# Edge features stored by the counting stage and loaded by the message stage of a graph network kernel

## The reference

```python
def _mlp(h, W, b, gamma, beta):
    h = jax.nn.relu(h @ W + b)
    mu = jnp.mean(h, axis=0)
    var = jnp.mean(jnp.square(h - mu), axis=0)
    return gamma * (h - mu) * jax.lax.rsqrt(var + EPS) + beta
node_feat = _mlp(x, W_node, b_node, g_node, beta_node)
edge_feat = _mlp(edge_attr, W_edge, b_edge, g_edge, beta_edge)
row, col = (edge_index[0], edge_index[1])
message = jnp.concatenate([x[row], x[col], edge_feat], axis=1)
message = _mlp(message, W_msg, b_msg, g_msg, beta_msg)
agg = jax.ops.segment_sum(message, col, num_segments=node_feat.shape[0])
return agg + node_feat
```

## Time and profile before

| | |
|---|---|
| median of 3 runs | 2815.78 us (2812.81 to 2824.91) |
| profiled execution | 2801.42 us, of which the span is 2799.7 |
| count_edges | about 57 to 600 us |
| pass_messages | about 1403 to 2621 us |
| busy share of the span | PE 66%, DVE 56%, POOL 33%, ACT 31% |
| mean granted clock of TensorE | 0.735 |

### The profile page before, as it was taken

The page is one execution under the profiler, slowest core; times in us unless marked ns, Lnnn a source line. Parts: engine busy times, 40 slices in busy tenths (PEclk is TensorE's granted clock), DMA queues, the critical chain, the costliest instruction groups (busy, mean ns, idle before and its releaser), DMA issues. The chain is left out here.

```text
span 2799.7 us, 50246 instructions
## 1 busy us (share of the span) xinstructions
PE 1853.1 (66%) x14611; PEld 1446.8 (52%) x14611; DVE 1564.5 (56%) x4031; ACT 861.7 (31%) x1484; POOL 936.1 (33%) x1182
## 2 busy tenths in 40 slices
PE   1777777779999999778525544544555555555488
PEld 0333444459999999745413433333444344333477
DVE  7856866665444444465434555555555555555753
ACT  1687566641111111121212222222222222222420
POOL 3311211131000000000166666666666666666100
PEclk9988988879999999889755555555555555555699
DMA  4211111110000000800132222222222222222200
GB/s 138 93 49 41 42 70 56 70 63 2 2 2 2 2 2 2 311 1 3 37 44 49 49 49 48 47 49 48 50 50 49 49 50 49 49 48 48 69 1 18
DMA packets 86652, 133.19 MB, mean 48 GB/s; under 512 B 48616, under 2 KB 55656, under 8 KB 86462
## 3 DMA queue, kind: packets, MB, share of 16 engines
q1 hardware_dynamic: 40398, 83.53, 8.8%
q0 software_dynamic: 25344, 38.98, 6.9%
q10 hardware_dynamic: 20720, 8.06, 1.3%
HBM read 95.89 MB, written 34.58 MB: 47 GB/s over the span
## 5 line engine op out<-in xcount | busy, mean ns | idle before, releaser
L1430 POOL DMA_INDIRECT counts<-p_rows,rows x784 | 745.6, 951 | 498.4 <-issue 224.0
L931 PE MATMUL ps_hop<-y,counts 128*128 128x192 f16 x6250 | 525.0, 247 | 21.6 <-DVEq L818 12.3
L1659 PE MATMUL ps_e_z<-e_w_q,counts 128*128 128x96 f32 x1568 | 364.1, 427 | 259.8 <-ACT counts L1595 219.9
L931 PEld LDWEIGHTS ps_hop<-y,counts 128*128 128x128 f16 x6250 | 520.0, 98 | 26.5 <-DVEq L818 12.4
L1659 PEld LDWEIGHTS ps_e_z<-e_w_q,counts 128*128 128x128 f32 x1568 | 341.8, 330 | 295.8 <-ACT counts L1595 249.9
L560 DVE TENSOR_TENSOR hot_w<-iota_w,places_now 128x1600 f16<-128x1600 f16 x300 | 297.0, 990 | 156.0 <-PE ps_counts L586 137.1
L586 PE MATMUL ps_counts<-hot_w,hot_p 128*128 x1196 | 287.6, 372 | 117.5 <-DVE hot_p L560 77.4
L1670 PE MATMUL ps_e_seg<-counts 128*128 128x192 f16 x784 | 140.7, 359 | 301.9 <-DVE counts L1470 151.1
L1670 PEld LDWEIGHTS ps_e_seg<-counts 128*128 128x128 f16 x784 | 100.4, 138 | 385.3 <-issue 198.2
L1595 ACT ACTIVATE counts<-ps_e_u 96x1024 f32<-96x1024 f32 x98 | 99.9, 1019 | 642.0 <-remote 591.1
L527 POOL TENSOR_TENSOR places_now<-places,origins (+1 forms) x302 | 115.4, 383 | 428.0 <-DVE hot_p L560 278.3
(11 more groups left out here) (401 smaller groups left out, 2483.4 us busy)
## 6 DMA issues: line engine op xcount, KB each, us to landing
counts<-count_rows SPq DMA_DIRECT2D x30, 800.0 KB, 6.6
count_rows<-attr_split SPq DMA_DIRECT2D x25, 800.0 KB, 3.8
counts<-p_rows,rows POOLq DMA_INDIRECT x784
e_attr<-attr_parts SPq DMA_DIRECT2D x99, 72.0 KB
attr_parts<-attr_split SPq DMA_DIRECT2D x9, 784.0 KB, 15.9
attr<-attr_parts SPq DMA_DIRECT2D x50, 140.6 KB
e_dst_rows<-dst_row SPq DMA_DIRECT2D x99, 64.0 KB
e_w_q<-q_rows ACTq DMA_DIRECT2D x392, 12.0 KB
```

What stands on the lines that cost most here:

```text
L931: mm = pe.matmul(ps[:, r, 0:2 * D], k.counts[:, m, b, :], y[:, odd, b, :], start=b == 0, stop=b == NB - 1)
L1430: nc.gpsimd.indirect_dma_start(z[:, slot, j, :], None, k.p_rows, bass.IndirectOffsetOnAxis(rows, 0)) \
L1659: mm = pe.matmul(ps_z[:, two, j // (STEP_TILES // 2), at:at + D], u_hot[:, two, j * P:(j + 1) * P], w_q[:, fed, j // Q_TILES, :], start=Tr ...
```

## The change

In the counting stage the relu of the edge features is kept. SP stores each unit's 96 x 2000 values (750 KB) in a new DRAM tensor u_rows when ACT has made them (`store`, after `u_taken`). ACT's next `rectified` waits for that store (`u_stored`) where it had waited for its own squares. The squares go to ps_u instead of u, so PE's next `edges` waits for `u_summed` instead of `u_taken`. POOL clears 352 columns of u once, and SP stores them as the padding. The early units are spread differently over blocks and over a block's windows, and SP's loop over the blocks is written out.

In the message stage e_attr, the two edge matmuls, the bank ps_e_u and ACT's relu are gone; SP loads 96 x 1024 values of u_rows (384 KB) into u_hot, which has three buffers. There are three pairs of banks for the messages, two banks for the sums (ps_e_u and ps_e_sq made room), and three buffers of place rows. PE issues messages(s+2) ahead of sums(s), and DVE adds the sums of s-2 in step s. The squares are reduced by one instruction over 128 x 768 and added to the totals in SBUF by a second. The split parts have a tensor of their own in SBUF.

```diff
-    EARLY = [7, 7, 6, 5, 5]
+    EARLY = [5, 4, 4, 4, 4, 3, 3, 3, 2, 2, 2]
+    U_PAD = TILES * P - E
...
-        u_done, u_taken, u_summed = sem("u_done"), sem("u_taken"), sem("u_summed")
+        u_done, u_taken, u_summed, u_stored = sem("u_done"), sem("u_taken"), sem("u_summed"), sem("u_stored")
...
-                return [(first + n, n + (d == 0)) for n in range(EARLY[d])]
+                return [(first + n, n * WINDOWS // EARLY[d] + (d == 0)) for n in range(EARLY[d])]
...
+            def store(n):
+                sp.wait_ge(u_taken, n + 1)
+                sp.dma_start(k.u_rows[:, bass.ds(n * (U_PARTS * U_EDGES), U_PARTS * U_EDGES)],
+                             u[:, :, :].rearrange("p a e -> p (a e)")).then_inc(u_stored, 16)
...
                     load(n)
+                    if not isinstance(n, int) or n:
+                        store(n - 1)
...
-            for_blocks(sp, one_block)
+            for d in range(NB):
+                one_block(d, d % 2)
+            store(U_UNITS - 1)
+            sp.wait_ge(u_stored, 16 * (U_UNITS + 1))
...
-                    pe.wait_ge(u_taken, n)
+                    pe.wait_ge(u_summed, n)
...
             def rectified(n):
                 act.wait_ge(u_done, n + 1)
-                if not isinstance(n, int) or n:
-                    act.wait_ge(u_summed, n)
+                act.wait_ge(u_stored, n * 16 + 16)
                 nc.scalar.activation(u[:, :, :], ps_u[:, :, 0:U_EDGES], ACT.Relu,
                                      accum_out=u_sums[:, 0, bass.ds(n, 1)]).then_inc(u_taken, 1)
 
             def squares(n):
                 act.wait_ge(u_taken, n + 1)
-                nc.scalar.activation(u[:, :, :], u[:, :, :], ACT.Square,
+                nc.scalar.activation(ps_u[:, :, 0:U_EDGES], u[:, :, :], ACT.Square,
...
+    ZS = MSG_HOTS = 3
+    SUMS = 2
...
-        attr = sb("e_attr", [PRODUCTS + 3, FED, STEP], BF16)
...
-        u_hot = room[:, hot_end:u_end].rearrange("p (a e) -> p a e", a=2)
-        split = room[:, u_end:split_end].bitcast(F16).rearrange("p (a j f) -> p a j f", a=2, j=STEP_TILES)
+        hot = room[:, z_end:hot_end].bitcast(F16).rearrange("p (a j s) -> p a j s", a=MSG_HOTS, j=STEP_TILES)
+        u_hot = room[:, hot_end:u_end].rearrange("p (a e) -> p a e", a=FED)
+        split = sb("e_split", [P, 2, STEP_TILES, 2 * D], F16)
...
-        ps_u = ctx.enter_context(nc.psum_tensor("ps_e_u", [D, 2, BANK], F32))
-        ps_z = ctx.enter_context(nc.psum_tensor("ps_e_z", [P, 2, 2, BANK], F32))
-        ps_s = ctx.enter_context(nc.psum_tensor("ps_e_seg", [P, BANK], F32))
-        ps_sq = ctx.enter_context(nc.psum_tensor("ps_e_sq", [P, BANK], F32))
-        sq_sum = ps_sq[:, 0:HALF_BANK]
-        ones_set, w_set = sem("ones_set"), sem("w_set")
+        ps_z = ctx.enter_context(nc.psum_tensor("ps_e_z", [P, ZS, 2, BANK], F32))
+        ps_s = ctx.enter_context(nc.psum_tensor("ps_e_seg", [P, SUMS, BANK], F32))
...
-                sp.dma_start(attr[0:PRODUCTS, fed, :], k.attr_parts[:, bass.ds(s * STEP, STEP)]).then_inc(landed, 16)
+                sp.dma_start(u_hot[0:D, fed, :], k.u_rows[:, bass.ds(s * STEP, STEP)]).then_inc(landed, 16)
...
-            sp.wait_ge(ones_set, 1)
...
                 dve.wait_ge(fed_in[fed], FEED * uses)
 
-                if s >= 2:
-                    dve.wait_ge(z_done, s - 1)
+                if s >= FED:
+                    dve.wait_ge(z_done, s - FED + 1)
...
-            def hots(s, two, places):
-                if s >= 2:
-
-                    dve.wait_ge(seg_done, s - 1)
+            def hots(s, places):
+                if s >= MSG_HOTS:
+
...
             def add_squares(s):
                 dve.wait_ge(squared, s + 1)
-                dve.wait_ge(sq_added, s + 1)
-                nc.vector.tensor_tensor(sq_sum, sq_sum, halves(z_sq)[:, 0, :], ALU.add).then_inc(sq_half, 1)
-                dve.wait_ge(sq_half, s + 1)
-                nc.vector.tensor_tensor(sq_sum, sq_sum, halves(z_sq)[:, 1, :], ALU.add).then_inc(sq_added, 1)
-
-            def low_part(two):
-                return nc.vector.scalar_tensor_tensor(by_half(split[:, two, :, D:2 * D]), by_tile(two), 0.0,
+                if s:
+                    dve.wait_ge(sq_added, s)
+                nc.vector.tensor_reduce(sq_step[:, :], squares_of(), AX.X, ALU.add).then_inc(sq_taken, 1)
+                dve.wait_ge(sq_taken, s + 1)
+                nc.vector.tensor_tensor(k.totals[:, 1, :], k.totals[:, 1, :], sq_step[:, :], ALU.add).then_inc(sq_added, 1)
...
-            nc.vector.memset(attr[:, :, :], 1.0).then_inc(ones_set, 1)
...
+            turned_hot(0, 0, 1, step_nodes(0))
+            hots(0, step_places(0))
+            turned_hot(1, 1, 1, step_nodes(1))
+            turned_hot(2, 2, 1, step_nodes(2))
             for s in range(STEPS):
-                add_rows(s, s % 2, s % SLOTS, s // SLOTS + 1)
-                if s:
-                    add_sums(s - 1)
+                add_rows(s, s % ZS, s % SLOTS, s // SLOTS + 1)
+                if s >= 2:
+                    add_sums(s - 2)
                 if s + 1 < STEPS:
-                    hots(s + 1, (s + 1) % 2, step_places(s + 1))
-                low_half(s, s % 2)
+                    hots(s + 1, step_places(s + 1))
+                low_half(s)
                 add_squares(s)
-                if s + 2 < STEPS:
-                    turned_hot(s + 2, s % 2, (s + 2) % FED, (s + 2) // FED + 1, step_nodes(s + 2))
+                if s + FED < STEPS:
+                    turned_hot(s + FED, s % FED, s // FED + 2, step_nodes(s + FED))
+            add_sums(STEPS - 2)
             add_sums(STEPS - 1)
-
-            dve.wait_ge(sq_added, STEPS + 1)
-            nc.vector.tensor_reduce(k.totals[:, 1, :], sq_sum.rearrange("p (j f) -> p f j", f=D), AX.X, ALU.add)
+            dve.wait_ge(sq_added, STEPS)
...
-            def edge_mlp(s, two):
-                act.wait_ge(u_done, s + 1)
-
-                if s >= 2:
-                    act.wait_ge(z_done, s - 1)
-                nc.scalar.activation(u_hot[0:D, two, :].rearrange("p (h e) -> p h e", h=2), ps_u[:, :, :], ACT.Relu) \
-                    .then_inc(u_ready, 1)
...
-            edge_mlp(0, 0)
-            edge_mlp(1, 1)
             for s in range(STEPS):
-                rectified(s, s % 2)
-                if s + 2 < STEPS:
-                    edge_mlp(s + 2, s % 2)
-
+                rectified(s, s % 2, s % ZS)
                 if s + FED < STEPS:
...
-            def edges(s, fed, uses):
+            def messages(s, at, fed, uses):
                 pe.wait_ge(fed_in[fed], FEED * uses)
-                if s:
-
-                    pe.wait_ge(u_ready, s)
-                for h in range(2):
-                    mm = pe.matmul(ps_u[:, h, :], k.w_edge[:, :], attr[:, fed, h * BANK:(h + 1) * BANK],
-                                   start=True, stop=True)
-                mm.then_inc(u_done, 1)
...
+                if s >= ZS:
+                    pe.wait_ge(z_low, s - ZS + 1)
...
-            def sums(s, two, slot):
+            def sums(s, bank):
                 pe.wait_ge(hot_ready, s + 1)
 
-                if s:
-                    pe.wait_ge(seg_joined, s)
+                if s >= SUMS:
+                    pe.wait_ge(seg_joined, s - SUMS + 1)
...
-            edges(0, 0, 1)
-            messages(0, 0, 0)
-            edges(1, 1, 1)
+            messages(0, 0, 0, 1)
+            messages(1, 1, 1, 1)
             for s in range(STEPS):
-                if s + 1 < STEPS:
-                    messages(s + 1, (s + 1) % 2, (s + 1) % FED)
                 if s + 2 < STEPS:
-                    edges(s + 2, (s + 2) % FED, (s + 2) // FED + 1)
-                sums(s, s % 2, s % SLOTS)
+                    messages(s + 2, (s + 2) % ZS, (s + 2) % FED, (s + 2) // FED + 1)
+                sums(s, s % SUMS)
```

97 lines of the change are left out of this document (45 added, 52 removed).

## The result

The changed kernel takes 2894.99 us (median of 4 runs, 2891.21 to 2898.75), the kernel before 2814.3 beside it. The ratio is 1.028, with a 95% interval of 1.0249 to 1.031: slower by 2.8%, where 3.5% faster was forecast, and outside the forecast's range. The profiled execution spans 2896.9 us against 2799.7, so 97.2 us have to be found.

What follows compares the result with a forecast made beforehand. The prediction took POOL's stops, ended late because TensorE completions arrive late, as the message stage's loss. Message stage -79, counting stage -17, start and end -5 sum to -101: 2715 us from a median of 2815.8, range 2570 to 2815.

Steps and rivals of the forecast that it cites:

- Message stage, -79 us: Message stage: TensorE two steps ahead makes POOL stop less often, 12.03 to 11.2 us a step over 95 steps.
- the first of the two lengths weighed: Message stage: three steps, 24 gathers, between POOL's stops of 4.1 us, 11.4 us a step; the other was four steps, 11.0.
- The picture of the lateness: Message stage: while gathers stream, TensorE completions arrive some 9.8 us late, one after another; a POOL stop releases all after 3.2 us.
- Start and end, -5 us: Message stage's start and end: two relus of 1.02 us, the e_attr memset of 2.62 and the final reduce of 0.55 go.
- Blocks 1 to 4, -28.7 us: Counting stage: ScalarE ends these blocks; 16 units instead of 23, at 4.1 us each, bring 139.60 us down to 111.
- Blocks 5 to 10, +10 us: Counting stage: nine added units, 37 us more of ScalarE, cost 10, between ends of 0 and 37.
- Stores, +2 us: Counting stage: 50 stores of 750 KB are hidden except for a block's first unit, at most 2 us in ten blocks.
- VectorE's step: Message stage: squares as one reduce of 0.93 us and an add of 0.3, 1.2 against 1.14; step stays 6.6 us.
- The feed: Message stage: the 384 KB u_hot load takes 3.2 to 6.6 us and is hidden; at most 19 us, taken as 0.
- rival B: Message stage: lateness covered whole, POOL never stops, -204 us; 2590 us in all, 2570 to 2620; chance 0.22.
- Rival D: Message stage: gathers lose pace beside a denser VectorE, 12.7 us a step, +62; 2856 us in all; chance 0.13.

Runs made afterwards that it cites:

- d3: Counting stage of the kernel before with the changed message stage, one 384 KB store at the end that every step loads; 2832.54 us, kernel before 2823.45.
- e0: d3 run once more on chip 7, same code; 2592.03 us, beside 2592.33 of the kernel before.
- d1: The changed kernel with the same 50 stores at 15 KB each in place of 750 KB; 2860.54 us, beside 2823.45 of the kernel before.
- d2: The changed kernel with its units planned as before, stores and waits as changed; 2919.76 us, beside 2823.45 of the kernel before.
- b1: The changed kernel without 49 of the 50 stores, each step loading the same piece; 2614.92 us, beside 2593.48 of the kernel before.
- b2: The changed kernel with feeds of 192 columns, 72 KB, instead of 1024, 384 KB; 2663.17 us, control 2669.29.
- c0: Control: the changed kernel with one register operation more in the counting stage; 2669.29 us, beside 2593.48 of the kernel before.

## Why the prediction was wrong, step by step

- **Message stage, -79 us**: it came as +19. The mechanism was right as far as the row length: cycles of 24 gathers, as in the first of the two lengths weighed. The term that failed is the stop. It was carried over from the earlier trace rows as 4.1 us, and measured 6.4 on the mean of 32. Of the 36.92 us of the cycle shown, 30.0 are gathers, about 5.7 the stop beyond the usual 0.30, and 1.15 a gather held at 2121.01. In the rows VectorE stands elsewhere when the flush comes, 1.5 us farther from the instruction that frees a slot; in most stops the flush is later as well, about 4 us after the last gather where it was 3.1. The step had assumed that nothing else changes when the row of gathers gets longer. In its last third it does: VectorE starts an instruction only each 1.4 us. Why is open, and one rival to VectorE's place was never tested: the stops' sum stayed at 196 to 204 us for the same gathers, as if each gather left a quarter of a microsecond to be made good, however the row is cut. The bounds of this term, -126 to -41, excluded a loss with no reason but the symmetry of the estimate.
- **The picture of the lateness**, completions that reach the others "some 9.8 us late, one after another", was read from rows of 16 gathers. In a row of 24 SyncE sees one 21.5 us late: it is late until the row ends, not for a length of its own. And the first of the two rows of the rest visit in the earlier trace rows doesn't show 9.8: VectorE's L1552 waits for that visit's own gathers as well, the last of which POOL ended at 1427.62; in the changed kernel the same wait (L1564) ends with their landing, at 1501.09, 6.8 us after the messages' listed end. There the sums, over at 1506.10, release VectorE at 1506.17 with gathers running beside, so a completion isn't always late while gathers stream.
- **That lateness was taken as a trait of the kernel.** It isn't: with the same message stage a step takes 12.2 us in d3 and 10.0 in e0, and the kernel before takes 2592 to 2596 us on three chips. The prediction could not know of them, but it could have left open how such a lateness answers to more load.
- **Start and end, -5 us**: none of it reached the time. SP's first feed does come 3.4 us earlier in the stage, without the memset, but the first gather starts at the same point as before, and the gathers and their stops account for the whole stage from there. Ahead of it the last store and its wait stand now: between SP's store of the last block and the first gather, 805.5 us before became 810.9. The forecast saw that store as one of fifty. Behind the last gather the changed kernel takes 213.3 us, and d1 and d2 with the same code there 207, so that these 7.6 us of the loss are not read as an effect.
- **Blocks 1 to 4, -28.7 us**: they gained 8, and 14 without stores (b1). With 16 units ScalarE is busy 93 of 131.6 us, TensorE 95 and VectorE 90: none is full, and which of them ends these blocks no run shows. The step took the whole of ScalarE's relief for time.
- **Blocks 5 to 10, +10 us**: they lost 37, and 33 without stores. ScalarE has 99 us of work there, TensorE 112 and VectorE 94, in 158 us. None is full, and yet the loss is as long as the upper end of the term, the whole of the added 37 us of ScalarE. That agreement is luck: the rows have 20 us of more work on TensorE and 17 of more waiting, for the load of a block's first unit above all, and the term priced neither. "ScalarE stays at 57 of 69 us" was an argument by busy share.
- **Stores, +2 us**: about 40 us by b1. The wait, which the forecast weighed, is small, as forecast (in d1 none is seen in blocks 11 to 24; in blocks 5 to 10 of the changed kernel ScalarE's relus wait 9.6 us for stores). What it left out is the volume: 750 KB in a block that before moved little more than its 800 KB. The table by stretch has it as GB/s, 64 before and 97 in the changed kernel, and the first could have been read, and the second worked out from it, ahead of the run.
- **VectorE's step**: the reduce takes 1.45 us (L1497), not 0.93; it is about what the step gave for a read twice as dear (0.36 + 576 x 2.0 ns = 1.5). Both forms that the price was read from read PSUM, and this one reads SBUF; what makes it dearer no run shows. It matters little: with prompt completions POOL still ends each step (10.0 us), and VectorE waits 2.8 us a step for the strips of L1604 (254.1 us in 90 steps).
- **The feed**: 3.7 us to landing on chip 11, within the 3.2 to 6.6 given, and b2 shows that its volume costs nothing where completions are prompt.
- **The rivals**: rival B's end of the message stage, no stop of POOL at 9.98 us a step, is what chips 4, 7 and 11 show, but there it is no gain, as e0 takes the time of the kernel before. Rival D (gathers that lose pace beside VectorE) didn't come: 0.94 to 0.95 us each, every 1.25 us. The slower outcome was given 0.12, nearly all to this one mechanism; the price of the counting stage's stores had no rival of its own.

The rule of the Trainium skill's page "SBUF — State Buffer", section "SBUF: two separate sides", cited with rival D, of gathers held while VectorE has the shared ports, shows in no run here: the gathers keep 10.0 us a step in c0, where VectorE is busy 637.38 of 900 us.

## What to carry to other kernels

A transfer that nobody waits for still costs what runs beside it: price its bytes against the traffic of the stretch, and not only the wait for its landing. Where a stage is a chain from window to window, moved work is not priced by the busy share of one engine: look at what it asks of each engine, at which window its load is issued, and who stands waiting then. Work taken away gives only what the next engine lets go. And a stall whose cause is not understood can't be priced by carrying its length over to another rhythm.
